# Two-layer sequence kernel on one core: the order, the banks and the stores of its last row, and the order at the seam between its two layers

## The reference

```
x = x + LayerNorm(Wout(gelu(Wsoma x) * sigmoid(Wtemp temporal(x))))      # first layer
x = x + Wo(attention(Wq x, Wk x, Wv x))                                  # second layer, 16 heads of 8
```

## Time and profile before

| | |
|---|---|
| Time, median of 3 runs | 358.99 us (357.45, 358.99, 360.57) |
| Time of the profiled execution | 357.64 us |
| Its span in the profile | 355.9 us |
| PE busy | 312.4 us (88%) |
| DVE busy | 294.2 us (83%) |
| POOL busy | 232.4 us (65%) |
| ACT busy | 212.8 us (60%) |
| Mean granted clock of PE | 0.964 |

### The profile page before, as it was taken

The page is one execution under the profiler, slowest core; times in us unless marked ns, Lnnn a source line. Parts: engine busy times, 40 slices in busy tenths (PEclk is TensorE's granted clock), DMA queues, the critical chain, the costliest instruction groups (busy, mean ns, idle before and its releaser), DMA issues. The chain is left out here.

```text
span 355.9 us, 10349 instructions
## 1 busy us (share of the span) xinstructions
PE 312.4 (88%) x3361; PEld 213.4 (60%) x3361; DVE 294.2 (83%) x1530; ACT 212.8 (60%) x452; POOL 232.4 (65%) x281
## 2 busy tenths in 40 slices
PE   1869559998998989898956889899999999999993
PEld 0526217565574656456442566777777777777782
DVE  4775997969697887969778987799999999999961
ACT  5753301575637355455621868788888888888872
POOL 3045144374655556374564787699999999999970
PEclk9989788999999999999986999999999999999998
DMA  6101000100001035300354045443454444301011
GB/s 202 57 0 32 0 0 2 30 4 29 2 0 31 1 75 85 49 0 0 55 69 56 0 65 112 108 125 90 109 112 127 100 120 100 77 3 34 3 32 30
DMA packets 23473, 18.91 MB, mean 53 GB/s; under 512 B 2304, under 2 KB 23040, under 8 KB 23424
## 3 DMA queue, kind: packets, MB, share of 16 engines
q1 hardware_dynamic: 23424, 18.31, 23.6%
HBM read 3.62 MB, written 2.10 MB: 16 GB/s over the span
## 5 line engine op out<-in xcount | busy, mean ns | idle before, releaser
L1423 POOL TENSOR_TENSOR arena<-arena,neg_max 128x512 f32<-128x512 f32 x128 | 129.6, 1039 | 15.2 <-DVE neg_max L1293 14.8
L1293 DVE CUSTOM_DVE_ANT_0 arena<-ps,arena 128x128 f32<-128x128 f32 x512 | 113.7, 286 | 8.5 <-issue 5.4
L942 ACT ACTIVATE arena<-ps 128x512 f32<-128x512 f32 x128 | 69.6, 597 | 9.4 <-PE ps L673 9.3
L673 PE MATMUL ps<-ident_sb,arena 128*128 128x128 f32 x512 | 68.2, 276 | 0.0
L673 PEld LDWEIGHTS ps<-ident_sb,arena 128*128 128x128 f32 x512 | 56.4, 141 | 7.0 <-POOL arena L1423 3.8
L1383 POOL TENSOR_TENSOR arena<-arena 128x448 f32<-128x448 f32 (+6 forms) x56 | 39.8, 711 | 29.8 <-DVE arena L1123 27.6
L1370 POOL TENSOR_TENSOR arena<-decay_a,arena 128x192 f32<-128x192 f32 x32 | 22.1, 710 | 41.4 <-ACT arena L805 41.4
L1293 DVE DVE_READ_ACCUMULATOR2_ANT neg_max<- 128x1 f32 x512 | 42.5, 83 | 0.1
L689 PE MATMUL ps<-arena 128*32 128x128 f32 x1024 | 41.2, 279 | 0.0
L1123 DVE TENSOR_TENSOR arena<-ps,arena 128x448 f32<-128x448 f32 (+6 forms) x56 | 23.6, 428 | 16.6 <-PE ps L460 9.9
L459 PE MATMUL ps<-mod_pa,lag_a 128*128 128x512 bf16 x64 | 26.2, 410 | 4.5 <-DVE arena L1123 3.0
(11 more groups left out here) (154 smaller groups left out, 595.0 us busy)
## 6 DMA issues: line engine op xcount, KB each, us to landing
arena<-q_parts SPq DMA_DIRECT2D x96, 64.0 KB
arena<-k_parts SPq DMA_DIRECT2D x96, 64.0 KB
arena<-in_x SPq DMA_DIRECT2D x8, 256.0 KB, 2.6
out<-arena SPq DMA_DIRECT2D x8, 256.0 KB, 3.3
w_sb<-in_w SPq DMA_DIRECT2D x1, 576.0 KB, 6.5
arena<-in_consts SPq DMA_DIRECT2D x1, 420.0 KB, 5.4
rows_sb<-in_rows SPq DMA_DIRECT2D x1, 288.5 KB, 2.9
ident_sb<-in_ident SPq DMA_DIRECT2D x1, 64.0 KB, 3.0
```

Source lines behind the costliest of these rows:

```text
L673: mm = pe.transpose(ps[1][:, q % 2, k * P:k * P + P], neg_t[q % NT_RING][:, k * P:k * P + P], ident)
L942: act.activation(probT[q % PT_RING], ps[1][:, q % 2, :], ACT.Exp, scale=-1.0)\
L1293: dve.tensor_tensor_reduce(out=neg_t[q % NT_RING][:, cs], in0=ps[0][:, score_bank(c) + slot, cs], in1=nbias[n % 2], scale=1.0, scalar=3.0e ...
L1423: pool.tensor_tensor(t4, t4, neg_max[:, n % 2, 4 * z:4 * z + 4].unsqueeze(2).broadcast_to([P, 4, P]), ALU.subtract).then_inc(s["shifted"], 1)
```

## The change

Four edits are joined.

1. The last row (31) gets its own PSUM banks: `turn_o`, `turn_attn` and `project` write to `ps[0]`, banks 0, 1 and 2. `turn_o(31)` no longer waits for the results of row 30; the order behind the loop is changed on PE, ACT and DVE.
2. The last store is split: rows 28 to 30 go when `result(30)` is done, row 31 by itself.
3. PE repeats a matmul whose result nobody reads, 14 times ahead of `b_locals(LAST, 1)` and 8 times ahead of `b_cross(LAST, 1)`.
4. DVE's order at the seam: `b_temporal` goes in front of `logits(2)`, and `logits(6)` and `logits(7)` go in front of the last `c_centre`.

```diff
+        def out_bank(n, k):
+            return ps[0][:, k, :] if n == B - 1 else ps[1][:, 3, :]
...
-            for g in range(G - 3, G):
+            for g in range(G - 3, G - 1):
                 store(g)
+            last = (G - 1) * GB
+            sp.wait_ge(s["y_ready"], last + GB - 1)
+            sp.dma_start(out_v[:, last:last + GB - 1, :], yout[(G - 1) % 2][:, 0:GB - 1, :]).then_inc(s["y_stored1"], 16)
+            sp.wait_ge(s["y_ready"], last + GB)
+            sp.dma_start(out_v[:, last + GB - 1:last + GB, :], yout[(G - 1) % 2][:, GB - 1:GB, :])\
+                .then_inc(s["y_stored1"], 16)
...
+            def repeat(times):
+                for _ in range(times):
+                    pe.matmul(bank(0, 2), lag_a[:, 0, :], mod_pa[1][:], start=True, stop=True)
...
                 b_carries(LAST, 1)
+                repeat(14)
                 b_locals(LAST, 1)
+                repeat(8)
                 b_cross(LAST, 1)
...
             def turn_o(n):
-                if n == 0:
+                if n == B - 1:
+                    pe.wait_ge(s["negt_ready"], 8 * 2 * B)
+                elif n == 0:
...
             over_octets(octet_step)                 # PE
+            values(2 * B - 1)
             turn_attn(B - 2)
-            values(2 * B - 1)
+            turn_o(B - 1)
             project(B - 2)
-            turn_o(B - 1)
             turn_attn(B - 1)
             project(B - 1)
...
             over_octets(octet_step)                 # ACT
+            move_o(B - 1)
             move_attn(B - 2)
-            move_o(B - 1)
             move_attn(B - 1)
...
                 c_residual(LAST, 0)                 # DVE, end()
+                b_temporal(LAST, 1)
                 logits(2)
-                b_temporal(LAST, 1)
                 logits(3)
                 b_mixed(LAST, 1)
                 logits(4)
                 logits(5)
                 c_moments(LAST, 1)
+                logits(6)
+                logits(7)
                 c_centre(LAST, 1)
...
-                if c + 3 < 2 * B:
+                if 1 <= c and c + 3 < 2 * B:
                     logits(2 * c + 6)
                     logits(2 * c + 7)
...
             over_octets(octet_step)                 # DVE
+            normalise(B - 1)
             result(B - 2)
-            normalise(B - 1)
             result(B - 1)
```

More of the change, by code:

```diff
@@ L352, in _ @@
                 store(g - 3)
-            for g in range(G - 3, G):
+            for g in range(G - 3, G - 1):
                 store(g)
+            last = (G - 1) * GB
[4 more added lines that the diff above has]
+                .then_inc(s["y_stored1"], 16)
             sp.wait_ge(s["y_stored0"], 16 + 16 * G // 2)
-            sp.wait_ge(s["y_stored1"], 16 + 16 * G // 2)
+            sp.wait_ge(s["y_stored1"], 32 + 16 * G // 2)
         @block.tensor
@@ L703, in turn_o @@
                 for o in range(2):
-                    mm = pe.transpose(ps[1][:, 3, o * P:o * P + P], oT[n % 2][:, o * P:o * P + P], ident)
+                    mm = pe.transpose(out_bank(n, 0)[:, o * P:o * P + P], oT[n % 2][:, o * P:o * P + P], ident)
                 mm.then_inc(s["on_ps"], 1)
@@ L708, in turn_attn @@
                 pe.wait_ge(s["attn_ready"], n + 1)
-                pe.transpose(ps[1][:, 3, 2 * P:3 * P], attn[n % 2], ident).then_inc(s["attnT_ps"], 1)
+                pe.transpose(out_bank(n, 1)[:, 2 * P:3 * P], attn[n % 2], ident).then_inc(s["attnT_ps"], 1)
             def project(n):
                 pe.wait_ge(s["attnT_ready"], n + 1)
-                pe.matmul(ps[1][:, 3, 3 * P:4 * P], attnT[n % 2], wt["wo"], start=True, stop=True).then_inc(s["y_ps"], 1)
+                pe.matmul(out_bank(n, 2)[:, 3 * P:4 * P], attnT[n % 2], wt["wo"], start=True, stop=True).then_inc(s["y_ps"], 1)
             def octet_step(c):
@@ L952, in move_attn @@
                 act.wait_ge(s["attnT_ps"], n + 1)
-                act.activation(attnT[n % 2], ps[1][:, 3, 2 * P:3 * P], ACT.Copy).then_inc(s["attnT_ready"], 1)
+                act.activation(attnT[n % 2], out_bank(n, 1)[:, 2 * P:3 * P], ACT.Copy).then_inc(s["attnT_ready"], 1)
             def octet_step(c):
@@ L1299, in normalise @@
                 dve.wait_ge(s["on_ps"], n + 1)
-                o = ps[1][:, 3, 0:2 * P].rearrange("p (h e) -> p h e", e=2 * DH)
+                o = out_bank(n, 0)[:, 0:2 * P].rearrange("p (h e) -> p h e", e=2 * DH)
                 dve.reciprocal(rden[:, n % 2, :], o[:, :, DH]).then_inc(s["rden_ready"], 1)
@@ L1315, in result @@
                     dve.wait_ge(s[f"y_stored{g % 2}"], 16 * (g // 2 + 1))
-                dve.tensor_tensor(yout[g % 2][:, b, :], ps[1][:, 3, 3 * P:4 * P], x1b_all[:, n, :], ALU.add)\
+                dve.tensor_tensor(yout[g % 2][:, b, :], out_bank(n, 2)[:, 3 * P:4 * P], x1b_all[:, n, :], ALU.add)\
                     .then_inc(s["y_ready"], 1)
```

## The result

The changed kernel takes 354.71 us in the median of 6 runs (354.01 to 356.20), the kernel before 359.15 us in 6 (357.45 to 360.57). The ratio is **0.9885, with a 95% interval of 0.9863 to 0.9908**: 4.1 us faster. The forecast was 355.7 us, 0.9% less.

The account below looks back on a forecast made before the run. POOL's full stretch, 230 to 345 us, keeps its pace, so only an earlier start (the seam) and a shorter end can win. 1.9 + 0.63 + 0.75 = 3.3 us off 358.99 gives 355.7 us, range 353.9 to 357.6.

Parts of the forecast that it names:

- The clock: Seam between the layers: 14 and 8 repeats fit PE's waits and keep full clock; DVE's line 1144 starts 0.91 us earlier.
- `b_temporal` ahead of `logits(2)`: DVE at the seam: `b_temporal` starts directly behind `c_residual`, 2.11 us earlier, only with the full clock.
- What is late next is PE's `b_out`.: Seam: `b_out` ends 0.27 us after DVE would be ready for `c_moments`, which then starts 1.84 us earlier.
- `c_residual` and POOL: End of the seam: `c_residual` loses 0.77 us to POOL's instructions; `logits(8)` then starts 1.9 us earlier.
- What `scores(5)` gains, all behind it gains.: Behind the seam: PE's chain from `scores(5)` is unbroken, the same work, so its 1.9 us carries through.
- The last row: Kernel's end: `values(63)` starts at 348.03 and `turn_o(31)`, with its own bank, 0.63 us earlier (0.4 to 0.85).
- The store: Last store, split: a quarter of the bytes flows behind the last row, 0.75 us less (bounds 0 and 0.9).
- The sum: Whole kernel: 1.9 + 0.63 + 0.75 = 3.3 us off 358.99, giving 355.7 us, 0.9% less.
- Rival (D): Seam and last row: `c_residual` runs free of POOL or `values(63)` starts at 347.9; 4.1 us gained, 354.9 us; chance 0.2.
- rival (A): Seam: the clock falls all the same in the 0.8 us gap; only 1.4 us gained, 357.6 us; chance 0.08.
- rival (B): Seam: clock already low at 181.4, the 14 repeats take 6.2 us; slower, 360.3 us; chance 0.03.

Follow-up runs that it names:

- e10: The changed kernel with filler matmuls ahead of `scores(5)` and 7 and 4 repeats instead of 14 and 8, against the kernel before: 355.32 us, ratio 0.9886.
- e8: The changed kernel with 28 instead of 14 repeats ahead of `b_locals`, against the kernel before: 355.64 us, ratio 0.9913.
- e2: The kernel before with DVE's new order at the seam alone, against the kernel before: 360.16 us, ratio 1.0033.
- e6: The changed kernel without its 22 repeats, against the kernel before: 357.99 us, ratio 0.9966.
- e3: The kernel before with the last row's order and banks alone and one whole store, against the kernel before: 358.29 us, ratio 0.9958.
- e4: The kernel before with the last store split alone, against the kernel before: 358.02 us, ratio 0.9953.
- e11: The changed kernel with filler matmuls ahead of `scores(5)` and both store parts issued behind the last result, against the kernel before: 354.71 us, ratio 0.9873.
- e9: The changed kernel itself run once more, against the kernel before: 353.92 us, ratio 0.9858.

## Why the prediction was right, and where it was off

- **The clock.** Right. 14 and 8 repeats hide in the waits, line 493's work takes 1.13 us, DVE goes on 0.90 us earlier (0.91 forecast). e10 and e8 bracket the count in their profiles: half as many let the clock fall, twice as many ahead of `b_locals` delay.
- **`b_temporal` ahead of `logits(2)`.** Right in size (2.17 us for 2.11) and in that it needs the full clock: e2 waits 1.20 us for the transposes. Not foreseen: with the low clock the order is a loss (e2, and e6 against e3 and e4).
- **"What is late next is PE's `b_out`."** Wrong. I let the two turns take too long; `b_out` started 1.08 us after `b_mixed`, not 1.37, and `c_moments` came 2.29 us after `b_mixed`, as before. This undercounts 0.28 us.
- **`c_residual` and POOL.** The mechanism held, the size didn't. The 1183 ns of the earlier trace rows are of the earlier `c_residual`, at 190.9 us; of the last one's four the second took 1125 ns before and takes 337 now. It is this that makes 2.45 us at `logits(8)` out of 1.66 at `c_residual`'s start. `c_residual` met only the last 0.36 us of POOL's pair (200.76 to 202.80) and took 1.22 us to the next start, hardly more than the 1.17 I had for it without any loss; I had let it lose 0.77. A wait of DVE for its own centring (0.21 us), which I had not counted, took part of that back. By the Trainium skill's rule of the exclusive lock (SBUF — State Buffer, Who interferes with whom) the four should be free once POOL is idle, and the trace agrees: 1.22 us to the next start, against 2.01 where a pair of POOL's ran beside them.
- **"What `scores(5)` gains, all behind it gains."** Right from `scores(6)` on, to 0.02 us. Wrong for the step between: I wrote that PE would be ready by 203.0 for 204.85 and put no price on that idle time. In the profiled execution it cost 1.55 us by the clock.
- **The last row.** 0.84 us for 0.63. `values(63)` starts 0.04 us behind ACT's exponentials and not 0.19; the chain behind `turn_o(31)` is unchanged at 2.31 us.
- **The store.** 1.1 to 1.3 us for 0.75. The trailing part of the landing shrank with the bytes, too: from the end of the flow to the end of the span it was about 1.5 us (354.4 to 355.9) and is about 1.0 (353.2 to 354.2). The estimate by the Trainium skill's fit (SBUF — State Buffer, The DMA setup-cost knee) was 0.45 us; the trace has 1.2, and here the measurement decides. The Trainium skill's advice in that section, the largest single transfer, isn't contradicted where the parts leave together: in e11 the split wins nothing (3.9 us, against 3.6 to 4.0 with one store).
- **The sum.** 1.9 + 0.63 + 0.75 = 3.3 us forecast, 2.45 + 0.84 + 1.2 = 4.5 us in an execution without the dip (e9's profile: 351.3 us). The medians have 4.4 us (5.2 in e9's round), the ratio 4.1. All three terms were sized low, and the dip was left out. In executions that have the dip the two errors work against each other, so the nearness of the 355.7 us to the 354.71 is in part luck. Rival (D), 4.1 us, was nearest, and both of its mechanisms were seen in part. The prediction gave "within 1%" 0.58 and "faster by over 1%" 0.4; the ratio is 0.9885, and its interval lies on both sides of 0.99. What rival (A) describes, a fall of the clock in the seam in spite of repeats, was seen at half the repeats (e10), rival (B) in no profile.

What stays open: what, in executions that were not profiled, makes the low stretch of the kernel before longer or shorter, and how often the dip behind `scores(5)` comes.

## What to carry to other kernels

An engine's wait that costs nothing by itself can cost through TensorE's clock: price each long wait of PE (in the first octets the clock fell behind a wait of 1.7 us in two of five profiles, in the seam behind 3.76 us) with what PE does next at half speed, and fill it if there is a bank that nobody reads. Reordering another engine's work is not neutral either, for it moves and lengthens such waits. A last store was worth splitting here only where the larger part left before the last result. And where one kernel's executions differ by 3 us, compare profiles from a common event on, not from the start of the span.

## What the runs showed of the hardware

- The granted clock after the same wait is not the same in each execution. With 1.70 us of PE waiting ahead of `scores(5)`, the clock fell to half 1 to 1.5 us behind the wait in two of five profiles (0.57 over 206 to 210 us in the changed kernel, 0.76 over 206 to 213 in e2) and stayed at 1.00 in three (e6, e8, e9). The low stretch of an unchanged seam lasted 10.2 us in the kernel before and 13.6 in e3, 1.2 us dearer.
- A kernel's executions differ by their mean granted clock: e6 ran in 354.9 us at 0.966 and 358.9 us at 0.947. Which stretch was low the mean doesn't say.
- Of four VectorE instructions on 128x128 values (line 1194, two inputs in SBUF), the second took 1125 ns while two of GpSimd's subtractions ran back to back, and 337 ns when they had ended.
- A store of 64 KB landed in 1.5 to 1.7 us, one of 192 KB in 2.0 to 2.1 us, those of 256 KB in 3.1 to 3.4 us in the median, but the 64 KB took 2.7 us when issued 0.41 us behind 192 KB.
